# A recurrent layer on one core: the products of queries and keys in quarter steps, and new hand-written orders of steps

## The reference, cut to what matters

```python
def wkv7(r, w, k, v, a, b):
    dT = jnp.exp(resh(w))
    def step(S, inp):
        rt, dt, kt, vt, at, bt = inp
        sa = jnp.einsum('bhij,bhj->bhi', S, at)
        S = S * dt[:, :, None, :] + sa[..., None] * bt[:, :, None, :] + vt[..., None] * kt[:, :, None, :]
        return (S, jnp.einsum('bhij,bhj->bhi', S, rt))
...
xn = _layernorm(x)
s = attn(xn)                     # token shift, six low-rank projections, wkv7, group norm, gate, output
g = silu(ffn(xn))                # gate and up to 768, silu(gate) * up, down to 256
return x + s * g
```

## Time and profile of the kernel before

| | |
|---|---|
| runs | 1598.40, 1603.26, 1605.24 us; median 1603.26 |
| profiled execution | 1603.78 us, of which the span of the profile is 1602.3 |
| granted TensorE clock, mean | 0.982 of full speed |
| busy: PE, DVE, ACT, POOL | 93%, 79%, 67%, 21% of the span |
| instructions in the span | 56437 |
| DMA | 58.37 MB, mean 36 GB/s |

### The profile page before, as it was taken

The page is one execution under the profiler, slowest core; times in us unless marked ns, Lnnn a source line. Parts: engine busy times, 40 slices in busy tenths (PEclk is TensorE's granted clock), DMA queues, the critical chain, the costliest instruction groups (busy, mean ns, idle before and its releaser), DMA issues.

```text
span 1602.3 us, 56437 instructions
## 1 busy us (share of the span) xinstructions
PE 1493.2 (93%) x24384; PEld 1028.5 (64%) x24384; DVE 1261.4 (79%) x2661; ACT 1073.9 (67%) x1889; POOL 335.8 (21%) x362
## 2 busy tenths in 40 slices
PE   3579999999999999899999989999999999999977
PEld 1256767576676767667676666757666675766755
DVE  2788888888888888788887878888888888878623
ACT  3658587585858758576775858768585876858412
POOL 3020301313040131302213030131304013130101
PEclk9799999999999999999999999999999999999979
DMA  4011120301112030110302112030111203011110
GB/s 149 14 21 21 35 47 17 62 19 40 28 35 47 17 62 19 33 34 24 58 16 46 35 21 47 17 62 19 40 36 32 42 17 62 20 40 28 34 34 28
DMA packets 251462, 58.37 MB, mean 36 GB/s; under 512 B 223696, under 2 KB 250704, under 8 KB 251088
## 3 DMA queue, kind: packets, MB, share of 16 engines
q1 hardware_dynamic: 241936, 41.95, 13.8%
q10 hardware_dynamic: 9280, 12.81, 2.2%
HBM read 36.38 MB, written 18.35 MB: 34 GB/s over the span
## 4 chain that ended last, share of the span: by engine, by line
PE 85%; DVE 6%; issue 2%; DMA 2%; ACT 2%; POOL 1%; SPq 1%; ACTq 0%; DVEq 0%; POOLq 0%
PE bank L536 21%; PE chunk L380 15%; PE bank L546 10%; PE bank L511 4%; PE bank L666 3%; PE chunk L644 3%; PE chunk L616 3%; PE chunk L591 3%; PE chunk L600 3%; PE bank L479 2%; PE bank L519 2%; PE bank L485 2%; DMA smalls<-in_x 2%; PE chunk L630 2%; PE bank L380 2%
## 5 line engine op out<-in xcount | busy, mean ns | idle before, releaser
L1327 POOL TENSOR_TENSOR SF<-ST,CT 128x256 f32<-128x256 f32 x128 | 84.1, 657 | 678.3 <-DVE ST L1213 678.3
L536 PE MATMUL bank<-xT,wg 128*128 128x256 f32 x768 | 202.8, 396 | 13.4 <-DVE VU L983 13.4
L536 PE MATMUL bank<-xT,wu 128*128 128x256 f32 x768 | 201.7, 395 | 4.6 <-DVE hT L1173 4.6
L546 PE MATMUL bank<-wd,hT 128*128 128x256 f32 x768 | 177.2, 384 | 0.9 <-DVE hT L1173 0.9
L536 PEld LDWEIGHTS bank<-xT,wg 128*128 128x128 f32 x768 | 139.2, 191 | 58.7 <-DVE VU L983 24.0
L546 PEld LDWEIGHTS bank<-wd,hT 128*128 128x128 f32 x768 | 144.5, 192 | 27.7 <-issue 7.4
L536 PEld LDWEIGHTS bank<-xT,wu 128*128 128x128 f32 x768 | 139.2, 191 | 34.1 <-issue 7.9
L380 PE MATMUL chunk<-KS,W 128*128 128x512 f32 x320 | 151.1, 603 | 2.3 <-ACT gT L721 2.3
L863 ACT ACTIVATE sg<-bank 128x512 f32<-128x512 f32 x96 | 57.2, 595 | 137.3 <-PE bank L536 125.6
L889 ACT ACTIVATE Y<-chunk 32x256 f32<-32x256 f32 x256 | 96.0, 375 | 50.1 <-PE chunk L600 47.3
L380 PE MATMUL chunk<-big,W 128*112 128x512 f32 (+1 forms) x256 | 121.9, 600 | 2.9 <-POOL big L1286 2.6
(11 more groups left out here) (157 smaller groups left out, 3230.1 us busy)
## 6 DMA issues: line engine op xcount, KB each, us to landing
smalls<-in_x SPq DMA_DIRECT2D x32, 256.0 KB, 3.0
Y<-in_x SPq DMA_DIRECT2D x32, 256.0 KB, 3.0
out<-fsil ACTq DMA_DIRECT2D x32, 256.0 KB, 2.2
scrA<-AM SPq DMA_DIRECT2D x64, 64.0 KB, 1.9
hat<-scrB SPq DMA_DIRECT2D x32, 128.0 KB, 3.1
hat<-scrF SPq DMA_DIRECT2D x32, 128.0 KB, 3.3
KE<-scrA SPq DMA_DIRECT2D x64, 32.0 KB, 2.1
scrT<-KE SPq DMA_DIRECT2D x16, 128.0 KB, 1.7
```

Of the source, the lines that this page charges most:

```text
L536: q = pe.matmul(o[:, TT_ * n2:TT_ * n2 + TT_], w[:, h, 128 * (n + n2):128 * (n + n2) + 128], x_now[:, h], start=(h == 0), stop=(h == NH - 1))
L546: q = pe.matmul(o[:, 256 * m:256 * m + 256], hT[:, n, 128 * m:128 * m + 128], wd[:, n, :], start=(n == 0), stop=(n == NF - 1))
L1327: pool.tensor_tensor(SF[:, :, :, :], ST[:, :, :, :], fade[:, c].unsqueeze(3).to_broadcast([128, B, NH, N]), ALU.mult).then_inc(*faded.up)
```

## The change

In PE's `pairs`, each quarter now yields after 16, 32 and 48 products, in place of once after 32, so that X in PE's strings stands for a step of 16 products. PE's strings have 8 X more in `ORDER` and in `FIRST` (12 become 20). All other letters have the same counts as before on each engine. All strings but one (`LAST` and `FIRST` of POOL, which stay) are laid out anew. What the steps compute, and the steps of all other streams, are the same.

```diff
-ORDER = {"pe": ("NNNFNKOOFNNOKVONNNNKVKRRBKBNNRNNNBBNBBVBNNBVBBNBBEBNBBVBBNBBVBXBBNNBXBBNBBXBXBBNBBNBXBBXNBBLBXBBNXBB"
-                "LXXXXLL"),
+ORDER = {"pe": ("NNNNFKOONFNOKKVNNNNOVKRRBKBNNRNNBBNNNBBVBNBVBBNBBEBNBBVBBNBVBBXXNBBNXBXBBXBBNBXBBNBXBNBXXBBXNBBLBXXB"
+                "BNXXBBLXXXXXXLL"),
...
@@ -510,8 +510,8 @@
                                     oc = o[p0:p0 + keys, 128 * n:128 * n + 128].rearrange("p (x e) -> p x e", e=L)
                                     q = pe.matmul(oc[:, :, BL * j:BL * j + BL], K[:, 2 * n + b, 64 * j + L * x:64 * j + L * x + keys],
                                                   Q[:, 2 * n + b, j, :, :, :].rearrange("p a b e -> p (a b) e"), start=True, stop=True)
-                        if n == 1:
-                            yield f"half{qt}"
+                        if n < QC // 2 - 1:
+                            yield f"part{qt}{n}"
                     q.then_inc(*ring.fill((t, "A", qt)))
                     yield f"matrix{qt}"
```

More of the change, by code:

```diff
@@ L51 @@
 CTOT = _at
-ORDER = {"pe": ("NNNFNKOOFNNOKVONNNNKVKRRBKBNNRNNNBBNBBVBNNBVBBNBBEBNBBVBBNBBVBXBBNNBXBBNBBXBXBBNBBNBXBBXNBBLBXBBNXBB"
-                "LXXXXLL"),
[L55 to L61, removed]
+ORDER = {"pe": ("NNNNFKOONFNOKKVNNNNOVKRRBKBNNRNNBBNNNBBVBNBVBBNBBEBNBBVBBNBVBBXXNBBNXBXBBXBBNBXBBNBXBNBXXBBXNBBLBXXB"
+                "BNXXBBLXXXXXXLL"),
+         "act": ("NFKFFFFNFFKVKNOKOVKKRBEBKRKXRXXDBNBVNBVBBVVBBBNVXBBBXBBBVBBBXXNBLBBXLBLBBXNBBLXX"),
+         "dve": ("ONOOBBBBBBBBODDBBBBBDBBFNBBDOKDKDEDKKXNEXDEKEEXXBXBXNXXBBEXXBXXBEXXXXBXXNXBXXBXBXLBBLXXXNXXXXXBBXXXL"
+                "BLXBBXLLLLLLLL"),
+         "pool": ("DBBBBBBLBBLBLLLLLLLL")}
+FIRST = {"pe": ("FNNKFNKNNNKNNRNVNNNVNNNKVNNKVRNNRNVVEXXXXXNXXXXXXLNXNNXXXXXXNNLXXLLNN"),
+         "act": ("FNNKFFFFKKNRFFVKVKKEKKNXXDVRRNVVVXVXXVNLXXLNXLXXLXN"),
+         "dve": ("DNDDNKNKFDEXKKEDDXEDDKEXXXXEXXXXXXXXNLXXXXXXXXLEEXXXNXXXXXXXXXLXLXLLLLLNLLL"),
          "pool": ("DLLLLLLLLLL")}
-LAST = {"pe": ("NNNNNONONNNOONNNBBNNNBBNBBBBBNBBBBBBNBBBBNBBBBBBNNBBBBBNBBBBNBBBBBBNBBNNNN"),
-         "act": ("NNNBBOBBBBOBBNBBBBBBBBNBNBBBBBBBBBNBN"),
-         "dve": ("BONOOBBBBBBBBBBBBBBBBONONBBBBBBBBNBBBNBBBBBNB"),
+LAST = {"pe": ("NOONNNNONNNONNNNBBNNBBBBBBBNBNBBBBNBBNNBBBNBBBNBBBBNBBBBNBBBBBNBBBBBNBBNNN"),
+         "act": ("NNNBBOBBOBBBNBBBBBBNBBBBBBBNBBBBBNBBN"),
+         "dve": ("OBOOBBBBBBBBBBBBBBNBBONNOBBBBBBBBBNBBBNBBBBNB"),
          "pool": ("BBBBBBBBB")}
```

## The result

| | before | changed |
|---|---|---|
| median of the runs | 1603.65 us (20 runs) | 1613.44 us (20 runs) |
| ratio, 95% interval | | 1.0059 [1.0036, 1.0083] |
| the same, beside the experiments | 1602.41 (29 runs) | 1615.24 (6 runs), 1.0090 [1.0058, 1.0122] |

The changed kernel is slower by 0.6 to 0.9%. The profile that came with the result is of a slow execution (1630.66 us, at a mean clock of 0.969), of a kind that both kernels have now and then and that the ratios leave out; the rows here are from a second profile of the same kernel, `after_again`, whose clock was 0.983 against 0.982 before and whose span is 1611.0 us.

A forecast was written before the change was run, and what follows sets the result against it. PE was taken as the bound, busy 91.4 of 93.1 us in a steady section. Terms -3 + 2 + 2 + 0 + 1 = +2 on the profiled 1603.78 us gave 1606 us, range 1593 to 1618.

The forecast's parts named there:

- the likeliest case: Whole kernel: 1606 us, no change beyond the 0.5% (8 us) that a measurement can tell; chance 0.50.
- rival 3: Inverse's flip to PE's L565: later flip uses up 0.9 us margin, PE waits 0.5 in 15 sections, +7, 1613; chance 0.13.
- My own sign of being wrong: A steady section under 92.0 us or over 94.5, or a change in DVE's 0.9 us wait before L536.
- Step 1: PE's L420 after L657: gate product fills the wait, part comes back at projection L380; -3 us, bounds -7.1 and 0.
- Step 2: PE's pair products in more places: one extra piece net per section at 0.13 us; +2 us, bounds 0 and +4.
- Step 3: Section 0: first keys come earlier, but L966 later, so L380 waits longer; +2 us, bounds -1.6 and +3.4.
- Step 4: Last two sections: new fillers around the chain of chunks, L1173 wait kept; 0, with 1 us either side.
- Step 5: Chain of chunks in steady sections: two more waits of L616 for the state; +1 us, bounds 0 and +4.
- Rival 4: ACT's added table load delays the gate tile for PE: 1.28 us in 15 sections, +19, 1625; chance 0.04.
- Rival 2: DVE's L1227 meets POOL's L1286 in more sections, 2.9 us each: 1615 for 5, 1644 for all; chance 0.13.
- Rival 1: Faster: all of L420's wait won, section 0 gains 1.6, L1227 collisions gone; 1591 us; chance 0.2.

The follow-up runs named there:

- experiment 5: Changed kernel with, on DVE alone, L989 moved behind the flip and the output of the second half; 1590.61 us, ratio 0.9932 to the kernel before.
- 6: Changed kernel with both output stores one letter earlier on ACT and L989 behind the flip on DVE; 1589.75 us, ratio 0.9925 to the kernel before.
- experiment 11: Kernel before with, on PE alone, one gate step (2 products) moved between L657 and L420; 1630.75 us, ratio 1.0140 to the kernel before.
- experiment 8: Changed kernel with both output stores earlier on ACT and quarter steps joined again into steps of 32 products; 1599.22 us, ratio 0.9988 to the kernel before.
- experiment 7: Changed kernel with output stores earlier, L989 behind the flip, and sections -1 and 0 ordered as in the kernel before; 1591.64 us, ratio 0.9947 to before.
- first_store_early: Changed kernel with only the first of a section's two output stores issued earlier on ACT; 1609.72 us, ratio 1.0049 to the kernel before.
- stores_early: Changed kernel with both output stores of a section issued one letter earlier each on ACT; 1595.15 us, ratio 0.9970 to the kernel before.

## Why the prediction was right or wrong

The range and its sense of "little changes, rather slower" held: 1613.44 lies in 1593 to 1618, 7 us above the number. But the likeliest case, no measurable change, was not what came: the ratio's interval excludes 1, and in the second comparison 0.5% as well. What came is rival 3, which I had given 0.13, at its place. That its price (1613) was met as well is luck. Without the waits at L565 the new order is at 0.9925 to 0.9932 (experiments 5 and 6), which makes about 1592 us by the ratio, 14 below my 1606. And the changed kernel is 20 to 26 us above that, where I had put 7. The two misses cancel for the most part. My own sign of being wrong came, too: a steady section longer than 94.5 us. The median is 94.6 in `after_again` and 94.7 in the other profile. (The 93.1 that I set beside it was one section; the median before is 93.5.)

**Rival 3, the flip.** That the margin would be used up by a later flip and an earlier PE was right: PE now arrives 6.5 us after the flip, and the loads take as long. The margin itself I had read too large. I added the page's median of 3.3 us to the second load's issue; in that very section the longer of the two took 3.8 (the issues of L1393 at 1258.0 and 1258.7 us in the kernel before):

```profile
DMA to landing us min/median/max: 3.3/3.5/3.8
```

So 0.4 us lay between the landing and L565 there and not 0.9, and over the steady sections 0.1 to 1.1, 0.8 in the median. What I missed is what else uses the path. I treated the load's 3.3 us as fixed, and looked at the order of SP, which hadn't changed. The output stores are on ACT's queue, and their times hang on ACT's order, in which a silu that waits for DVE had come to stand ahead of them. So "a little slower" was 0.9 to 1.4 us a section on average (12.3 and 19.6 us in 14 sections) where I had put 0.5, and what I held unlikely was the rule.

**Step 1, L420.** The wait fell from 7.1 to 1.2 us, and the projection in front of which 0.3 us was to come back is about 0.2 us later than its own shortest distance in the steady sections. So -3 had about its size. But the reason was incomplete: by itself the edit costs 22 us (experiment 11), since the place of a step in the ring moves, too. I had named this as "the gate tile is needed some products later", and had the table load for a free extra; it looks like a condition of the gain.

**Step 2, the visits.** +2 was predicted, and neither the times nor the profiles of experiment 8 can tell its sign. Pieces of 32 records take 0.35 to 0.45 us, as I had said, with 0.67 for 64 and 1.20 for 128. By these the fixed part of a visit is 0.05 to 0.13 us, so that 0.13 was its upper end; it was read from pieces with different neighbours. The prediction gave nothing for the small waits that a finer step can fill, and that term stays open.

**Step 3, section 0.** Its size, +2, is what the medians of the profiles show (178.7 to 181.0 us at the start of section 2, experiment 7), within a spread of 4 to 6 us, but not its mechanism: L380's wait for L966 fell instead of growing (5.4 to 4.3 us in two places; predicted longer by some 1.3), L511's for the keys fell by 1.4, and the new wait of 6.6 us is L485 for ACT's evictions, an engine that I hadn't looked at in that section.

**Step 4, the end.** Taken as 0 within 1; by the profiles it's some -4 to -5. The 4.6 us wait for L1173, of which I said that the new order keeps it, is gone.

**Step 5, the chain.** +1 predicted; L616's wait for the state is 3.8 us in 7 places against 4.3 in 8, L644's for DVE fell from 3.7 to 0.7. The chain lost nothing and gained a few us.

**Rival 4, the table load,** didn't come: PE waits for no silu in the changed kernel. **Rival 2,** L1227 beside L1286, happened in 2 sections before, in 4 and in 0 sections in two executions of the same changed kernel, 0 to 3 in the others. So much of it is a lottery of the execution, which I hadn't allowed for; whether the order weighs in it can't be told from these. Its price was too low as well: the four sections with a slow L1227 in `after_again` are 2.1 to 6.3 us longer than the median, 3.4 on average, where I had taken 2.9 from PE's wait alone. The longest is explained by the clock (last section below).

**Rival 1** didn't come. The repaired kernel of experiment 5 is at 0.9932, about where this rival was (1591), but by other parts: L420's waits fell, the end and small waits gained, while section 0 lost.

## What to carry to other kernels

When a change moves steps on one queue, list for each chain through memory (store, load, first use) what other transfers leave within its time, on every queue and in whatever engine's order they wait; the margin in front of the first use tells whether they matter. Take the margin from the landings of all sections, and not from a median of the page. A margin of under 1 us on an engine that hardly ever waits is a resource: two changes that are each free within the noise cost a per cent together, and moving one instruction behind the flip brought more than the whole rewritten order. And a step that takes a tile of a ring moves every later step's tile: ask who empties the tile that the next user now gets.

## What the runs showed of the hardware

- A store of 128 KB on SP's queue (scrT<-KE) took 1.7 us to land, and 2.5 when ACT's store of 256 KB had left 0.2 us before it; where they left at the same time, the 128 KB landed after 1.7 us again, and SP's next load (L1393) left late instead, 3.0 to 3.6 us after L1385 and not 2.5. So tenths of a microsecond between two queues told who was late. The loads themselves took longer with an output store near: from the issue of L1393 to the landing of its second load 4.05 us in the median before, 4.55 and 4.83 with the store 0.2 us behind (two profiles of the changed kernel), and 4.89 with it 0.5 us behind (`first_store_early`).

Its row with the output store early (`stores_early`: KB each, us from issue to landing):

```profile
scrT<-KE SPq DMA_DIRECT2D x16, 128.0 KB, 1.7
```

and in `after_again`:

```profile
scrT<-KE SPq DMA_DIRECT2D x16, 128.0 KB, 2.5
```

- The collision of DVE's L1227 with POOL's L1286 (4.97 instead of 1.43 us) hit no section in one execution of the changed kernel and four in another.

- Such a meeting can cost more than the wait that it makes. In `after_again`, PE was idle for 2.8 us ahead of the L657 of 585.4 us. The granted clock, 1.00 until then, was at 0.50, the lower of its two levels (1.2 GHz), from about 586 to 595 us, with PE busy throughout (2 us of that: length, PE busy, clock, DMA):

```profile
586.00:588.00 2.00, 2.00 (x9) 0.50 0.00 0
```

That section lasted 100.9 us, 6.3 more than the median. In the section with a slow L1227 from 756.3 us the mean granted clock stayed at 1.00, and it was 2.1 us longer.
